# Two-layer transformer kernel: front of the second attention two sequences ahead, scores of two heads in row halves

## The chip, the cores and the metric

One core of one Trainium2 chip. The metric is the device time of the whole program in microseconds. A core has TensorE (PE; its weight loads stand apart as PEld), VectorE (DVE), ScalarE (ACT), GpSimd (POOL) and SyncE (SP), each with its own queue of instructions, and 16 DMA engines. Matmuls write to PSUM, eight banks of 512 f32 columns on 128 partitions.

## What is computed

16 sequences of 512 tokens and 128 channels, everything in f32, go through two layers. Each layer adds an attention and a feed-forward to its input:

```python
xn = layernorm(x)
x  = x + attn_A(xn) + block_B(xn)      # layer 0
xn = layernorm(x)
x  = x + flash_attn(xn) + fp4_ffn(xn)  # layer 1

# attn_A: 16 heads of 64; the mask keeps key position <= row position
k = einsum('ahe,bce->bach', W_K, x); q = einsum('ahe,bce->bach', W_Q, x); v = ...
scores = einsum('bach,baCh->bacC', k, q)            # rows are keys' tokens here
attn = softmax(masked(tril(scores)) / sqrt(64))
z = einsum('bach,bacC->baCh', v, attn); out = W_O z

# block_B: x + attn (layernorm, causal convolution of 3 taps, 16 heads of 8, rotary), then
#          x + mixture of 4 experts, each token uses the expert of its largest logit
# flash_attn: 16 heads of 8, blocks of 64 with a running maximum
# fp4_ffn: inputs and weights rounded to 4-bit values in groups of 16, gate/up/down 352 wide
```

## The kernel before

**Three parts of three sequences at a time.** The work on a sequence is cut into three parts, and `pipeline` runs them side by side for neighbours: in one call of `run(i, nxt, prv)` the sequence `i` is in its *dense* part (attn_A and the experts), `nxt` is in its *ahead* part (block_B's layernorms, convolution, second attention, router) and `prv` in its *behind* part (layer 1). The calls are one with `nxt` alone, one for sequence 0, a hardware loop (`Fori(1, B - 1)`, 14 passes), one for sequence 15 and one with `prv` alone. A period is one such call.

**Order by hand.** Every engine walks the same list in `walk`. The dense part has 129 places (0 to 63: 16 heads times four query tiles; 64 to 127: 16 chunks of the experts in four steps each); `PLACES` hangs the steps of the other two parts at places. Semaphores say what must be done; within an engine the order is the list's.

**First attention (dense, places 0 to 63).** For each head h, `key_side` projects `mg[h]` (W_Q and W_K multiplied in the preparation) with `xnTd` to a 128 x 512 tile in bank 3 (L1282); ACT copies it to `gs` (L661). Then four tiles t follow, with widths 128, 256, 384 and 512: a matmul of all 128 rows (L1325) into bank `pos % 3` and a bf16 mask matmul on its last 128 columns (L1327); DVE takes the row maxima (L976), ACT the exponentials and their sums (L681). The bank is free for the tile three places on when ACT is through. Every other head `value_side` projects v for a pair (L1273, bank 3, evacuated at L655); DVE inverts the sums (L937), POOL scales v (L550), and `values` multiplies (L1293, bank 4): the two heads of a pair write to partitions 0 to 63 and 64 to 127 of the bank, 64 columns of the array each. L1354 is the output projection `ao`.

**Experts (dense, places 64 to 127).** Per chunk a gate matmul (L1339), tanh on ACT (L694), two DVE operations (L947, L952) around a value matmul (L1346); the sums of each expert at L1305 and L963.

**Front of the second attention (ahead).** `load_x` (a DMA on ACT's queue into `xin`), `ln0_*`, `transpose0` (`xn` into `xnT`, later copied to `xnTd` at L645), `ln1_apply`, `transpose1`, `conv`, `project_q`/`project_k` with the rotation (two matmuls into banks 5 and 6), `split_q`/`split_k` (each value as a sum of three bf16 parts in `part`), and then 18 DMAs of 128 KB on POOL's queue (`send_stack`, L572), behind a tiny POOL operation each (L568), into `qst` and `kst`. These steps hang at places 1 to 12. `row_max` (44 units, L1399, L1401, L1041, banks 5 and 6) needs all 18 transfers and hangs at places 28 to 68; `shift_rows`, `exps` (44 units, L1418, L1420, L727) and `attend` (L1433, four heads in column quarters) lie in the expert places; then `divide`, `join`, `project_y`, `ln3_*`, `transpose3` (L1262), `route` (L1463).

**Behind.** `take_over` (L1096), `ln2_*`, `transpose2`, `keys1`, `queries1`, `values1`, `scores1`, `block_max1`, `shift1` (L1120), `sum1` (L1128), POOL's `totals1`, `blend1`, `weigh1`, then `probs_T1`, `mix1` (L1519), the 4-bit rounding (`round_x`, `round_h`) and `gate1`, `up1`, `transpose_hq`, `down1`. The result is stored by a DMA on ACT's queue (L790), and DVE waits for its landing at the end of the call.

## Time and profile before

| | before |
|---|---|
| median of 3 runs | 3992.66 us (3991.66 to 3997.45) |
| the profiled execution | 3994.44 us |
| its span, first to last instruction | 3992.6 us |
| PE busy | 3586.5 us (90%), 20335 matmul records |
| DVE busy | 2576.8 us (65%) |
| ACT busy | 1802.0 us (45%) |
| POOL busy | 608.3 us (15%) |
| mean granted clock of PE | 0.936 |

Times are in us unless marked ns; "L1325" is a line of the kernel. An f32 matmul stands as two records. The end of a matmul is modelled and lies behind its last column, so neighbouring records overlap: what a matmul costs is read from its start to the start of the next. The granted clock is 1 at 2.4 GHz and 0.5 at 1.2 GHz. "issue" as a releaser is idle time in which the engine waited for nothing that the profile shows.

### The profile page before, as it was taken

Reading aid. Unit: us, or ns where it says so; the run is one execution under the profiler, and the core shown is the slowest. Engines: PE = TensorE matmul, PEld = TensorE weight load, DVE = VectorE, ACT = ScalarE, POOL = GpSimd, SP = SyncE. Lnnn points to the kernel's source line nnn. Section 1 sums busy time; section 2 is a strip of 40 time slices with the busy share of each in tenths; the row PEclk is TensorE's granted clock in tenths of the full one; section 3 lists DMA queues with packets and bytes.
Section 4 is the critical chain, followed back from the end, with each engine's and each line's share of the span. In section 5 each row is a group of like instructions: output and inputs, shape, how many; then the busy total and the mean of one; then the engine's idle time right before and its main releaser. Section 6 shows DMA issues by size and latency. Waiting matters only on the chain.

```text
span 3992.6 us, 66986 instructions
## 1 busy us (share of the span) xinstructions
PE 3586.5 (90%) x20335; PEld 2096.9 (53%) x20335; DVE 2576.8 (65%) x6166; ACT 1802.0 (45%) x4300; POOL 608.3 (15%) x1188
## 2 busy tenths in 40 slices
PE   3799998999999899999989999998999999899974
PEld 2355554555555455555555555555555555555542
...
GB/s 98 4 25 4 25 2 31 2 13 19 6 27 2 31 2 7 25 5 27 2 31 2 7 25 5 27 2 31 2 12 20 5 28 2 31 2 4 1 3 3
DMA packets 51980, 59.15 MB, mean 15 GB/s; under 512 B 19634, under 2 KB 41076, under 8 KB 51572
## 3 DMA queue, kind: packets, MB, share of 16 engines
...
## 4 chain that ended last, share of the span: by engine, by line
PE 79%; DVE 9%; issue 6%; ACT 3%; POOL 2%; DMA 1%; SPq 1%; ACTq 0%; DVEq 0%; POOLq 0%
PE ps L1325 13%; PE ps L1282 6%; PE ps L1339 6%; PE ps L1293 6%; PE ps L1346 5%; PE ps L1305 5%; PE ps L1433 4%; PE ps L1418 4%; PE ps L1399 4%; PE ps L1273 3%; PE ps L1519 3%; PE ps L1497 3%; PE ps L1354 3%; PE ps L1513 1%; PE ps L1420 1%
## 5 line engine op out<-in xcount | busy, mean ns | idle before, releaser
L681 ACT ACTIVATE share_a<-ps,nma 128x128 f32<-128x128 f32 (+3 forms) x1024 | 539.1, 528 | 547.2 <-DVE nma L976 536.3
L1325 PE MATMUL ps<-share_g,xnTd 128*128 128x128 f32 (+3 forms) x2048 | 757.7, 467 | 30.6 <-ACT share_a L681 16.7
L976 DVE TENSOR_REDUCE nma<-ps 128x1 f32<-128x128 f32 (+3 forms) x1024 | 490.7, 488 | 397.9 <-PE ps L1327 382.5
L727 ACT ACTIVATE share_z<-ps 128x512 f32<-128x512 f32 (+1 forms) x704 | 369.3, 558 | 497.4 <-PE ps L1420 494.2
L1041 DVE TENSOR_REDUCE nmx<-ps 128x1 f32<-128x384 f32 (+3 forms) x704 | 427.0, 635 | 122.7 <-PE ps L1401 117.9
L1325 PEld LDWEIGHTS ps<-share_g,xnTd 128*128 128x128 f32 x2048 | 343.0, 198 | 267.7 <-issue 138.7
L947 DVE SCALAR_TENSOR_TENSOR share_g<-share_g,ps 128x512 f32<-128x512 f32 x256 | 175.3, 685 | 405.3 <-ACT share_g L694 403.4
L550 POOL TENSOR_TENSOR vn<-va,rla 128x256 f32<-128x256 f32 x256 | 160.3, 627 | 1277.7 <-DVE rla L937 1277.5
L1282 PE MATMUL ps<-xnTd,mg 128*128 128x512 f32 x512 | 307.4, 685 | 23.1 <-ACT va L655 23.1
L1293 PE MATMUL ps<-share_a,vn 128*64 128x512 f32 (+3 forms) x2048 | 309.8, 445 | 18.3 <-POOL vn L550 18.3
L577 POOL TENSOR_TENSOR share_s<-q1T,tab 128x1024 f32<-128x1024 f32 x16 | 30.4, 1899 | 1768.7 <-ACT q1T L755 1768.7
L1399 PE MATMUL ps<-kst,qst 96*128 96x128 bf16 (+3 forms) x1024 | 263.8, 311 | 29.1 <-DMA kst<-share_r 25.1
L1339 PE MATMUL ps<-h2Td,wgv 128*128 128x512 f32 x512 | 272.2, 613 | 19.0 <-ACT share_a L681 19.0
L1346 PE MATMUL ps<-h2Td,wgv 128*128 128x512 f32 x512 | 266.6, 602 | 0.0
L1418 PE MATMUL ps<-qst,kst 99*128 99x512 bf16 (+3 forms) x1024 | 255.1, 303 | 8.3 <-DMA qst<-share_h 4.2
L1293 PEld LDWEIGHTS ps<-share_a,vn 128*64 128x64 f32 x2048 | 138.0, 138 | 225.0 <-issue 192.1
L1305 PE MATMUL ps<-wdn,share_a 128*128 128x128 f32 x2048 | 251.9, 278 | 1.3 <-DVE share_a L952 1.3
L1305 PEld LDWEIGHTS ps<-wdn,share_a 128*128 128x128 f32 x2048 | 237.4, 192 | 13.4 <-issue 7.4
L1327 PE MATMUL ps<-up_b,ident_b 128*128 128x128 bf16 x1024 | 228.8, 223 | 0.0
L694 ACT ACTIVATE share_g<-ps 128x512 f32<-128x512 f32 x256 | 153.4, 599 | 124.8 <-PE ps L1339 123.8
L1401 PE MATMUL ps<-up_b,ident_b 128*128 128x128 bf16 x1024 | 202.8, 225 | 0.0
L655 ACT COPY va<-ps 128x512 f32<-128x512 f32 x128 | 74.7, 583 | 280.1 <-PE ps L1273 280.1
...
## 6 DMA issues: line engine op xcount, KB each, us to landing
qst<-share_r POOLq DMA_DIRECT2D x144, 128.0 KB, 7.3
kst<-share_r POOLq DMA_DIRECT2D x144, 128.0 KB, 12.7
xin<-in_L_attn_x ACTq DMA_DIRECT2D x16, 256.0 KB, 2.7
out<-xn ACTq DMA_DIRECT2D x16, 256.0 KB, 2.3
...
```

What stands on the lines that cost most here:

```text
L681: activation(pa[:, h % 4, OFF[t]:OFF[t] + P * (t + 1)], ps[:, pos % 3, 0:P * (t + 1)], ACT.Exp, bias=nma[:, h, t:t + 1], accum_out=la[:, h ...
L727: activation(pt[:, n % 2, h % 4:h % 4 + k, 0:wd], src, ACT.Exp, scale=SCALE_B)\
L976: v.tensor_reduce(nma[:, h, t:t + 1], ps[:, pos % 3, 0:P * (t + 1)], AX.X, ALU.max, negate=True).then_inc(amax, 1)
L1041: v.tensor_reduce(nmx[:, h:h + k, t], src, AX.X, ALU.max, negate=True).then_inc(bmax_ready, 1)
L1282: mm(ps[:, 3, :], mg[:, h, :], xnTd[:, :], start=True, stop=True).then_inc(g_psum, 1)
L1293: ins = mm(ps[DA * k:DA * k + DA, 4, 0:P * (t + 1)], vn[:, h % 4, t, :], pa[:, h % 4, OFF[t]:OFF[t] + P * (t + 1)], start=(t == NT - 1), s ...
L1305: ins = mm(ps[:, 3, tile(t)], ym[:, e % 2, c, tile(t)], wdn[:, e, c, :], start=(c == 0), stop=(c == CHUNKS - 1))
L1325: mm(ps[:, b, 0:P * (t + 1)], xnTd[:, tile(t)], gs[:, h % 2, 0:P * (t + 1)], start=True, stop=False)
L1339: mm(ps[:, (2 * n) % 3, :], wgv[:, e, c * P:(c + 1) * P], h2Td[:, :], start=True, stop=True).then_inc(gate_psum, 1)
L1346: mm(ps[:, (2 * n + 1) % 3, :], wgv[:, e, DFF + c * P:DFF + (c + 1) * P], h2Td[:, :], start=True, stop=True).then_inc(value_psum, 1)
L1399: mm(ps[:, b, o:o + wd], qst[0:SHIFT_ROW, h, tile(t)], kst[0:SHIFT_ROW, h, 0:wd], start=True, stop=False)
L1418: mm(ps[:, b, o:o + wd], kst[0:SHIFT_ROW + PARTS, h, tile(j)], qst[0:SHIFT_ROW + PARTS, h, j * P:T], start=True, stop=False)
```

## The change

**Pipeline.** A fourth part, *early*, is cut off the front of *ahead*: `load_x`, `ln0_*`, `ln1_apply`, `transpose1`, `conv`, `project`, `split` and the 18 stack transfers are done for the sequence two ahead (`nn`). `run(i, nxt, nn, prv)` is called once with `nn` alone, once with `nxt` and `nn`, for sequences 0 and 1, in the loop `Fori(2, B - 2)` (12 passes), for 14 and 15, and with `prv` alone.

**Order.** `PLACES` and the 129 places are gone; one list `ORDER` holds the steps of all four parts, the dense ones too. The early steps now stand among the expert steps; `row_max` 0 to 43 among the scores of pairs 1 to 7.

**First attention per pair.** The preparation keeps W_K and W_Q transposed (`wkqT`) and no product. Keys and queries of a pair of heads are projected in two matmuls (128 x 512 each) into two banks and copied together by one ACT operation 1024 wide. A unit of scores is a tile t of both heads: head 0 multiplies rows 0 to 63, head 1 rows 64 to 127 of the pair's `kq`, each into its own bank, then two mask matmuls. One DVE reduction takes both heads' maxima, two ACT operations the exponentials. The four banks 0 to 3 are a ring of two slots of two banks, through which projections and scores go in turn. `v` goes through bank 4, which it shares with `values`; one reciprocal and one POOL operation per pair take the place of two.

**Buffers and queues.** `xnT` and its copy go: `xn` is kept by a DMA in `xk`, transposed late in the period (`turn_x`) and written straight to `xnTd`. `hc`, `part`, `xres` and `kq_odd` have memory of their own (`kq_odd` doubles as `rope`). The loads of x (one into `xin`, one into `xres`), the 18 stack transfers, the copy to `xk` and the store of the result are on SP's queue; POOL and ACT issue no DMA. The wait for the store's landing moves from the end of DVE's call to the next `ln2_apply`.

```diff
-            run(None, (0, 0), None)
-            run((0, 0), (0, 1), None)
-            with eng.Fori(1, B - 1) as i:
-                run((i, 0), (i, 1), (i, -1))
-            run((0, B - 1), None, (0, B - 2))
-            run(None, None, (0, B - 1))
+            run(None, None, (0, 0), None)
+            run(None, (0, 0), (0, 1), None)
+            run((0, 0), (0, 1), (0, 2), None)
+            run((0, 1), (0, 2), (0, 3), (0, 0))
+            with eng.Fori(2, B - 2) as i:
+                run((i, 0), (i, 1), (i, 2), (i, -1))
+            run((0, B - 2), (0, B - 1), None, (0, B - 3))
+            run((0, B - 1), None, None, (0, B - 2))
+            run(None, None, None, (0, B - 1))
...
+RING = [("kq", 0), ("kq", 1)]
+for _p in range(PAIRS):
+    RING += [("scores", _p, _t) for _t in range(NT)] + ([("kq", _p + 2)] if _p + 2 < PAIRS else [])
+RING_AT = {unit: n for n, unit in enumerate(RING)}
...
+ORDER = [
+    ("take_over",), ("begin",), ("kq", 0), ("v", 0), ("kq", 1), ("ln2_stats",), ("scores", 0, 0), ("v", 1),
+    ("scores", 0, 1), ("ln2_root",), ("project_v",), ("scores", 0, 2), ("scores", 0, 3), ("ln2_apply",),
+    ("kq", 2), ("scores", 1, 0), ("transpose2",), ("scores", 1, 1), ("norm", 0), ("scores", 1, 2), ("keys1",),
+    ("z", 0), ("queries1",), ("row_max", 0), ("row_max", 1), ("values1",), ("v", 2), ("row_max", 2),
...
+    ("kq", 4), ("running_max1",), ("shift1", 0), ("scores", 3, 0), ("shift1", 1), ("shift1", 2), ("scores", 3,
+    1), ("norm", 2), ("row_max", 15), ("scores", 3, 2), ("z", 2), ("v", 4), ("shift1", 3), ("sum1", 0),
+    ("sum1", 1), ("sum1", 2), ("scores", 3, 3), ("sum1", 3), ("totals1", 1, 4), ("totals1", 4, 8), ("kq", 5),
+    ("row_max", 16), ("row_max", 17), ("row_max", 18), ("scores", 4, 0), ("row_max", 19), ("scores", 4, 1),
+    ("norm", 3), ("ratios1",), ("blend1", 7, 4), ("scores", 4, 2), ("blend1", 3, 0), ("row_max", 20),
+    ("row_max", 21), ("weigh1", 0), ("weigh1", 1), ("z", 3), ("row_max", 22), ("row_max", 23), ("v", 5),
+    ("scores", 4, 3), ("row_max", 24), ("row_max", 25), ("kq", 6), ("row_max", 26), ("row_max", 27),
+    ("probs_T1", 0, 0), ("weigh1", 2), ("scores", 5, 0), ("row_max", 28), ("scores", 5, 1), ("norm", 4),
...
+    ("round_h", 3, 3), ("round_h", 3, 4), ("ln3_root",), ("ln3_apply",), ("down", 3), ("acc", 3),
+    ("transpose_hq", 3), ("down1",), ("transpose3",), ("route",),
+]
...
# SP
+                def split(z):
+                    if z == 0 and nxt is not None:
+                        sp.wait_ge(bst_psum, count(nxt, AHEAD["bst_psum"], UNITS))
+                    stack = (qst, kst)[z]
+                    for a in range(PARTS):
+                        sp.wait_ge(split_ready, count(nn, EARLY["split_ready"], 3 * z + a + 1))
+                        for b in range(PARTS):
+                            r = DB * (PARTS * a + b) if z == 0 else DB * (PARTS * b + a)
+                            sp.dma_start(stack[r:r + DB, :, :], part[:, z, a, :]).then_inc(stack_loaded, 16)
...
# TensorE
+                def ring_turn(*unit):
+                    n = RING_AT[unit]
+                    if n >= 2:
+                        kind, p, *t = RING[n - 2]
+                        if kind == "kq":
+                            pe.wait_ge(kq_ready, count(i, DENSE["kq_ready"], p + 1))
+                        else:
+                            pe.wait_ge(aexp_done, count(i, DENSE["aexp_done"], 8 * p + 2 * t[0] + 2))
...
+                    return 2 * (n % 2)
+                def project_kq(p):
+                    if p == 0:
+                        pe.wait_ge(xnTd_ready, count(i, DENSE["xnTd_ready"], 1))
+                    b = ring_turn("kq", p)
+                    for z in range(2):
+                        ins = mm(ps[:, b + z, :], wkqT[:, z, 2 * DA * p:2 * DA * (p + 1)], xnTd[:, :],
+                                 start=True, stop=True)
+                    ins.then_inc(kq_psum, 1)
...
+                def scores(p, t):
+                    if t == 0:
+                        pe.wait_ge(kq_ready, count(i, DENSE["kq_ready"], p + 1))
+                    b = ring_turn("scores", p, t)
+                    for k in range(2):
+                        rows = slice(DA * k, DA * k + DA)
+                        mm(ps[:, b + k, 0:P * (t + 1)], kq[p % 2][rows, 0, tile(t)], kq[p % 2][rows, 1, 0:P * (t + 1)],
+                           start=True, stop=False)
+                    for k in range(2):
+                        ins = mm(ps[:, b + k, tile(t)], ident_b[:, :], up_b[:, :], start=False, stop=True)
+                    ins.then_inc(as_psum, 1)
...
-                        mm(ps[:, b, 0:P * (t + 1)], xnTd[:, tile(t)], gs[:, h % 2, 0:P * (t + 1)],
-                           start=True, stop=False)
-                        mm(ps[:, b, tile(t)], ident_b[:, :], up_b[:, :], start=False, stop=True).then_inc(as_psum, 1)
...
# VectorE
+                def scores(p, t):
+                    dve.wait_ge(as_psum, count(i, DENSE["as_psum"], 4 * p + t + 1))
+                    b = 2 * (RING_AT["scores", p, t] % 2)
+                    v.tensor_reduce(nma[:, 2 * p:2 * p + 2, t], ps[:, b:b + 2, 0:P * (t + 1)],
+                                    AX.X, ALU.max, negate=True).then_inc(amax, 1)
...
# ScalarE
+                    for k in range(2):
+                        h = 2 * p + k
+                        activation(pa[:, h % 4, OFF[t]:OFF[t] + P * (t + 1)], ps[:, b + k, 0:P * (t + 1)], ACT.Exp,
+                                   bias=nma[:, h, t:t + 1], accum_out=la[:, h, t:t + 1]).then_inc(aexp_done, 1)
```

## Rows read from the trace of the kernel before

**Rows 1.** The page, section 1: busy us, share of the span, instructions.
```profile
PE 3586.5 (90%) x20335; PEld 2096.9 (53%) x20335; DVE 2576.8 (65%) x6166; ACT 1802.0 (45%) x4300; POOL 608.3 (15%) x1188
```
**Rows 2.** The page, section 4: shares of the chain that ended last.
```profile
PE 79%; DVE 9%; issue 6%; ACT 3%; POOL 2%; DMA 1%; SPq 1%; ACTq 0%; DVEq 0%; POOLq 0%
```
**Rows 3.** The chain in order of time: start us, us, what; L1354.
```profile
1706.59 7.15 PE ps L1354 x64
1939.50 7.15 PE ps L1354 x64
```
**Rows 4.** Busy time by stretch: attention, experts, seam, prologue.
```profile
core 0: us, PE busy (x) PEld busy (x) DVE busy (x) ACT busy (x) POOL busy (x), PEclk, DMA share, GB/s
2028.00:2160.00 132.00, 123.10 (x632) 70.04 (x632) 97.41 (x227) 68.92 (x184) 37.21 (x73) 0.97 0.20 21
2160.00:2258.00 98.00, 93.48 (x635) 58.04 (x635) 62.76 (x157) 42.84 (x85) 0.70 (x1) 0.99 0.02 5
2021.00:2040.00 19.00, 11.26 (x43) 7.00 (x43) 11.65 (x55) 5.25 (x12) 0.00 (x0) 0.73 0.08 23
51.00:181.00 130.00, 76.55 (x448) 31.27 (x449) 48.17 (x107) 29.24 (x55) 12.56 (x24) 0.67 0.20 19
```
**Rows 5.** Timeline of PE, scores of one head: start us, us, what.
```profile
2085.91 1.08 PE L1325 MATMUL ps<-share_g,xnTd 128*128 128x512 f32 x2
2086.82 0.22 PE L1327 MATMUL ps<-up_b,ident_b 128*128 128x128 bf16 x1
2086.93 0.48 PE L1325 MATMUL ps<-share_g,xnTd 128*128 128x128 f32 x2
2087.25 0.22 PE L1327 MATMUL ps<-up_b,ident_b 128*128 128x128 bf16 x1
```
**Rows 6.** Timeline of PE, the values of one pair.
```profile
2102.78 0.22 PE L1327 MATMUL ps<-up_b,ident_b 128*128 128x128 bf16 x1
2102.93 2.38 PE L1293 MATMUL ps<-share_a,vn 128*64 128x512 f32 x16
2105.23 0.34 PE L1399 MATMUL ps<-kst,qst 96*128 96x384 bf16 x1
```
**Rows 7.** Groups by line and shape: busy us, mean ns, idle before, releaser.
```profile
L976 DVE TENSOR_REDUCE nma<-ps 128x1 f32<-128x512 f32 x256 | 176.6, 690 | 100.9 <-PE ps L1327 95.0
L976 DVE TENSOR_REDUCE nma<-ps 128x1 f32<-128x128 f32 x256 | 73.5, 287 | 120.5 <-PE ps L1327 115.9
L681 ACT ACTIVATE share_a<-ps,nma 128x512 f32<-128x512 f32 x256 | 175.7, 686 | 263.4 <-DVE nma L976 263.4
L681 ACT ACTIVATE share_a<-ps,nma 128x128 f32<-128x128 f32 x256 | 95.1, 371 | 56.5 <-DVE nma L976 53.3
L681 ACT ACTIVATION_READ_ACCUMULATOR share_a<-ps,nma 128x1 f32 x1024 | 201.0, 196 | 0.0
```
**Rows 8.** Timeline of PE at a seam in the loop; last line: the first seam.
```profile
2024.12 1.05 PE L1463 MATMUL ps<-wrt,share_h 128*128 128x4 f32 x8 [0.87 <-ACT share_h L741]
2028.29 2.07 PE L1273 MATMUL ps<-wvT,xnTd 128*128 128x128 f32 x8 [3.12 <-issue]
2031.04 2.07 PE L1282 MATMUL ps<-xnTd,mg 128*128 128x512 f32 x2 [0.68 <-ACT va L655]
...
2039.76 0.65 PE L1262 MATMUL ps<-ident,xn 128*128 128x128 f32 x4 [1.68 <-DVE xn L844]
...
383.82 1.14 PE L1273 MATMUL ps<-wvT,xnTd 128*128 128x128 f32 x8
```
**Rows 9.** Waits: engine, line, waited for, us in total, times, longest.
```profile
PE ps L1399 <- DMA kst<-share_r: 25.1, 2, 23.8
PE ps L1293 <- POOL vn L550: 18.3, 5, 7.5
...
POOL qst L572 <- issue: 17.0, 3, 7.8
```
**Rows 10.** The page, section 6: DMA issues, KB each, us to landing.
```profile
qst<-share_r POOLq DMA_DIRECT2D x144, 128.0 KB, 7.3
xin<-in_L_attn_x ACTq DMA_DIRECT2D x16, 256.0 KB, 2.7
```

659 lines of the change are left out of this document (327 added, 332 removed), and 10 rows, old and new, of tables (ORDER, PLACES).

## Prediction

> **What bounds the kernel now.** I read the page's busy shares first: TensorE (PE) is busy 90% of the span, VectorE (DVE) 65%, ScalarE (ACT) 45% [rows 1]. A busy PE need not be the bound, so next the chain of work that ended last: 79% of it is PE, 9% DVE [rows 2]. So I sum PE time. The steady state repeats: the output projection of the first attention (64 records, L1354) starts every 233 us [rows 3]; sixteen of these are 93% of the time. Three stretches of one period come next [rows 4]: the attention stretch (132 us: PE 123, DVE 97), the expert stretch (98 us: PE 93, DVE 63), and the seam between two sequences (19 us: PE only 11.3, granted clock 0.73). At two levels, 2.4 and 1.2 GHz, a mean of 0.73 means that a good half of those 19 us ran at the lower one. So there are two things to win: PE work inside the period, and the seam.
>
> **Scores in row halves.** An f32 matmul stands as two records. 64 records of 128 columns take 7.15 us [rows 3], so 0.223 us for 128 columns and 2.23 us for the 1280 columns of one head's four tiles (128+256+384+512). Measured by starts, a head takes 0.91 us for its 512-column tile and 0.32 us for its 128-column tile [rows 5], which lies nearer to 2.4 for the head. Two heads, one after the other, are then 4.46 to 4.80 us; the masks (0.06 us each, same number) stay. The nearest row for two half-array matmuls side by side is the product with the values (L1293), which lies in column halves: eight f32 matmuls, 2560 columns, the same number as two heads of scores. They start 0.15 us after a mask where 0.06 is usual, and the next instruction starts 2.30 us later [rows 6]: 2.39 us, not 4.46. So halves do run side by side, and a visit to the split array costs about 2.39 - 2.23 = 0.16 us (up to 0.26 if I take a faster column rate). After the change the rows are halved and not the columns, an operation that the trace does not show. There are four visits per pair and not one, because the full-array masks stand behind each tile. A pair costs 2.23 + 4 x 0.16 = 2.87 us at best, 2.13 + 4 x 0.26 = 3.2 us at worst. Saved: between 1.3 and 1.9 us per pair; I take 1.45, since a short visit can hide less of its weight load. 16 sequences of 8 pairs: 186 us (range 165 to 245). The new projections `project_kq` have 2 x 512 columns per pair, as had the two `key_side`: nothing.
>
> The Trainium skill ("TensorEngine Tiling (Array Packing)", Tiling Modes, Key Properties) says that changing the tiling mode drains the TensorE, which speaks against four visits per pair; the 0.09 us of late start in rows 6 agrees with a drain of that size. The same page allows row halves to run independently if they write different PSUM banks (Gotcha 1), as here; no row shows that yet.
>
> **The ring of score banks.** Before: three banks, one head each. After: two slots of two banks, and the projections take slots too. A slot is free when both heads' exponentials are through. Price of a slot's return: a reduce of both heads (128 columns 0.29, 512 columns 0.69 us, so 0.42 to 1.23 us for double width by that slope), then two exponentials with their accumulator reads (0.46 to 0.78 us each by start) [rows 7], plus some 0.35 us of PE drain (a 0.06 us mask stands as 0.22, rows 5) and hops: 1.7 us for tile 0, 3.2 us for tile 3. Beside it PE has one other unit (0.6 to 1.2 us) and what the order puts between. I walked pair 4 and 5 of the new order: between tile 0 and tile 2 of pair 4 there are only one `row_max` (0.28) and tile 1 (0.8), against 1.7 plus a DVE queue: 0.7 us of idle. Pair 3 has `shift1` and `sum1` on DVE (eight operations 1024 wide, about 1.2 us each by the same slope) and 13.7 us of DVE against 10.6 of PE: some 3 us. Pair 5 comes through without a wait. DVE in the attention stretch after the change: 97 (rows 4) + 2 (the last `row_max`) - 5 (eight pairs of 3.3 for 3.9 us) - 16 (`ln0`, convolution, rotation and splits leave, some 24 operations of 0.4 to 0.7 us and 30 small ones beside) = about 78 us of about 115, so DVE binds only where its work is bunched. I price the ring at +4 us per sequence against 1 to 2 now; ends: 1 (the walk counts waits that other work fills) and 10 (each pair waits 1.2 us).
>
> **The seam.** Now [rows 8]: 0.87 us for the activation in front of the router, then 3.12 us with nothing to wait for, then 0.68 us for the evacuation of v (a like one of g follows) and 1.68 us for `ln2_apply`. The 3.12 us are there only in the loop: at the first, unrolled seam the same L1273 follows with no idle [rows 8]. It is the jump back, and the change keeps a loop (12 passes, not 14), so 3.1 us stay. `xnTd` no longer comes through two copies behind the route; `kq` 0, `v` 0 and `kq` 1 stand in a row (4.4 us), so the waits for v and g go. But tile 2 of pair 0 and `kq` 2 wait for DVE, which has `route`, `take_over`, `begin`, `ln2_stats` and `ln2_root` (about 8 us of small operations) in front of the reductions: I count 2 to 4 us. The idle stays near 8 us; denser work behind it should bring the clock back some 3 us of work earlier. The output store and the waits behind it leave ACT and the end of DVE's run, which gives little: the DVE idle there is the jump. I take 4 us per seam won, less the 2.5 us of the ring: net 2.5 us with the rest of the period's small waits, 16 times: 40 us.
>
> **The front two sequences ahead.** `ln0`, convolution, rotation, splits and 18 stack transfers per sequence move from the attention stretch into the expert stretch, where DVE has room (63 of 98 us) [rows 4]. PE does the same matmuls. The stack goes from POOL's queue to SP's. SP waits there for the last `exps`; behind it in its queue stand the copy `xk` and the output store, neither needed before the next `turn_x` and `ln2_apply`. The transfers (128 KB, 7.3 us each for the queries, overlapping) [rows 10] made PE wait 23.8 us in the prologue [rows 9]; from the last `exps` to the next `row_max` 0 I count about 50 us of PE work. Hidden; without that cover up to 24 us a sequence. POOL also loses its long idle pieces at the transfers, with no releaser shown (17.0 us in three at the query stack alone); behind them PE waited for POOL's `vn` for 18.3 us in sum [rows 9]: I take 15 us.
> The prologue grows: sequence 0's front runs alone as now, but sequence 1's front is now in the stage behind it. There the PE clock is 0.67 and DVE is busy 48 of 130 us [rows 4], so most of some 20 us of DVE work hides: +12 us (0 to 20), of which the end gives back nothing, since the last period is set by other work. The tail, the second block of the last sequence alone, has no part in the change.
>
> **Sum.** The profiled execution has a span of 3992.6 us and 3994.4 us in all, 1.8 around it; the median shown is 3992.7. 3994 - 186 - 40 - 15 + 12 = 3765 us.
>
> **Rivals.**
> A. The halves don't overlap, or the mode change eats the gain (slower). Row halves are not column halves: if both heads' partial sums go down the same columns one after the other, a pair costs 4.46 + 4 x 0.16 = 5.1 us, 2.1 more than the forecast pair of 3.0 to 3.1, 128 times: 270 us, so 4035. The same side is reached from 0.56 us per visit (2.23 / 4). Against it: rows 6. Its neighbour: the stack transfers on one queue one after the other (18 x 7.3 = 131 us against 50 of cover), which would cost over 50 us a sequence; against it, a 256 KB load on ACT's queue lands in 2.7 us [rows 10]. 11% together.
> B. The ring binds: each pair waits 1.2 us more, and DVE with its bunches keeps PE from running ahead: +6 us per sequence, 3860. For it: two slots, and `row_max` in front of reductions. 18%.
> C. Better: visits at 0.16, serial heads at 2.4, the walk's waits filled, clock at the seam up. 40 us more from the scores, 4 us a period: 3665. 14%.
> D. The change of place matters nothing and the scores give half, since a short tile's weight loads show: 3870 to 3950, close to B. 4%, with 2% of no change at all.
> The forecast's own case: 51%, 3700 to 3820.
>
> **How the numbers follow.** 3765 is the likeliest. The range reaches over B and most of C and leaves A out: 3660 to 3925. One measurement of this kernel can tell about 0.2% from no change. Faster by more: the forecast, B, C and D, 0.87; within: 0.02; slower: 0.11.
>
> **What would show it.** Scores: the two heads' records start within some ns of each other, and a pair of tiles of 128 to 512 columns with its masks takes 3.3 to 3.7 us. If the second head starts only when the first is through, A. Ring: PE's waits for the exponentials and evacuations of the first attention come to 40 to 100 us in sum; over 150 is B. Seam: about 8 us idle in 19, the 3.1 us still there in the loop. Period: 219 us, not 233. Stack: no PE wait for `kst` beyond the prologue's. DVE near 155 us of 219. The prediction is wrong in kind if a period stays above 230 us.

## The result, and the profile after

The changed kernel takes 3896.1 us (median; 3885.1 to 3904.0) beside 3992.2 us of the kernel before: a ratio of 0.9756, 95% interval 0.9743 to 0.9768. That is 96 us less. The forecast was 3765 us, 227 us less: the sign and the range held, the size did not. The profiled execution of after took 3885.1 us (span 3883.0). It is the fastest of its four, 11 us under the median, at a mean granted clock of 0.941 where the other three have 0.937; the one of before took 3994.4 us.

The busy shares of the page, which answer to [rows 1]:

```profile
PE 3406.5 (88%) x20319; PEld 1876.6 (48%) x20319; DVE 2506.9 (65%) x5526; ACT 1754.1 (45%) x4156; POOL 381.3 (10%) x676
```

PE lost 180 us of busy time, the span only 110: PE was busy for 90% of the span and now for 88%. POOL lost 227 us, DVE 70.

Next one period in one window. Columns as in [rows 4]; idle is the width less PE's busy time. First before, from one value projection (L1273) to the next:

```profile
core 0: us, PE busy (x) PEld busy (x) DVE busy (x) ACT busy (x) POOL busy (x), PEclk, DMA share, GB/s
2491.90:2724.50 232.60, 219.32 (x1268) 129.54 (x1268) 158.55 (x383) 111.98 (x268) 37.92 (x74) 0.96 0.12 14
```

232.6 us, of which PE idles 13.3. Three periods of after, from one output projection (L1403) to the next:

```profile
1647.20:1871.90 224.70, 208.12 (x1268) 115.58 (x1267) 154.46 (x343) 108.89 (x259) 23.82 (x42) 0.97 0.11 17
1871.90:2100.90 229.00, 211.38 (x1269) 116.60 (x1268) 154.67 (x344) 108.90 (x259) 23.83 (x42) 0.96 0.12 16
2100.90:2323.70 222.80, 205.57 (x1269) 114.91 (x1268) 154.42 (x344) 108.85 (x259) 23.83 (x42) 0.98 0.12 17
```

They are 224.7, 229.0 and 222.8 us wide, with 16.6, 17.6 and 17.2 us idle. Counted from one sequence's first value projection (L1349) to the next one's, the ten periods behind the loop's first pass have a mean of 225.8 us; the forecast was 219. In the three windows PE is busy for 8 to 14 us less in a period, at a granted clock of 0.96 to 0.98 (0.96 before), and idles 3 to 4 us more, where the forecast had it idle less. In 15 periods 136 us are won. The first value projection starts at 201.2 us instead of 181.2, so the prologue gives back 20 us (12 forecast), and the end 6.

The scores, PE's timeline, one tile of 512 columns and one of 128, each for both heads of a pair (as [rows 5], where each was one head):

```profile
2486.95 1.13 PE L1359 MATMUL ps<-kq_odd 64*128 64x512 f32 x4
2488.01 0.29 PE L1362 MATMUL ps<-up_b,ident_b 128*128 128x128 bf16 x2
2488.14 1.94 PE L1337 MATMUL ps<-xnTd,wkqT 128*128 128x512 f32 x4
...
2491.44 0.22 PE L1462 MATMUL ps<-up_b,ident_b 128*128 128x128 bf16 x1
2491.59 0.49 PE L1359 MATMUL ps<-share_g 64*128 64x128 f32 x4
2492.01 0.29 PE L1362 MATMUL ps<-up_b,ident_b 128*128 128x128 bf16 x2
2492.14 0.38 PE L1460 MATMUL ps<-kst,qst 96*128 96x512 bf16 x1
```

From start to start a wide tile of both heads with its two masks is 1.19 us and a narrow one 0.55 (two heads, one after the other, by [rows 5]: 2 x 1.02 and some 2 x 0.43). The halves overlap. Behind another mask a tile starts 0.15 us after it where 0.06 is usual, as in [rows 6]. With the two tiles between (0.76 and 0.97) and four late starts of 0.09 a pair takes 3.82 us; the prediction looked for 3.3 to 3.7.

The seam in the loop, PE, ACT and DVE (answers to [rows 8]; the last bracket is the idle time in front and what ended it):

```profile
2418.39 1.06 PE L1524 MATMUL ps<-wrt,share_h 128*128 128x4 f32 x8 [0.87 <-ACT share_h L777]
...
2422.65 3.53 PE L1337 MATMUL ps<-xnTd,wkqT 128*128 128x512 f32 x4 [3.21 <-issue]
...
2429.33 0.62 ACT L692 COPY h2Td<-share_h 128x512 f32<-128x512 f32 x1 [10.99 <-issue]
...
2430.99 0.49 PE L1359 MATMUL ps<-share_g 64*128 64x128 f32 x4 [2.19 <-ACT share_g L703]
...
2431.62 0.43 DVE L1147 COPY xp<-xacc 128x512 f32<-128x512 f32 x1 [10.19 <-issue]
```

PE waits behind the jump as before (3.21 us, 3.12 then). New is that ACT's and DVE's first instructions behind it come 10.99 and 10.19 us late, also without a releaser. The evacuation of `kq` 0 stands behind ACT's, so `scores` 0,0 (L1359) waits 2.19 us. The 19 us around this jump, and the same 19 us of the kernel below that sends the transfers from POOL, to be set beside the third row of [rows 4]:

```profile
2415.30:2434.30 19.00, 12.73 (x66) 8.35 (x66) 7.08 (x33) 3.71 (x5) 0.00 (x0) 0.87 0.53 79
1490.60:1509.60 19.00, 14.64 (x80) 9.23 (x78) 9.84 (x46) 6.79 (x15) 0.00 (x0) 0.82 0.22 50
```

PE idles 6.3 us in the one and 4.4 in the other, against 7.7 before, at a clock of 0.87 and 0.82 against 0.73. In the mean of ten seams it is 7.3 us before, 6.0 after and 4.2 with POOL's transfers. So the seam itself did get better; the jump's late engines took back some 2 us of it.

Waits (engine, what, for whom: us in sum, times, longest), which answer to [rows 9]:

```profile
PE ps L1359 <- ACT share_a L718: 56.8, 70, 1.9
PE ps L1337 <- issue: 47.3, 11, 11.8
PE ps L1460 <- DMA kst<-part: 36.4, 1, 36.4
PE ps L1376 <- POOL vn L614: 35.0, 48, 1.8
...
PE ps L1337 <- ACT share_a L718: 22.8, 16, 1.9
...
ACT h2Td L692 <- issue: 111.0, 11, 11.0
...
DVE xp L1147 <- issue: 100.7, 11, 10.3
```

The copies behind the jump waited 10.1 and 9.2 us in the mean, in each of 11 passes; before it was 38.4 us in 13 for DVE. PE's longest wait at the jump, 11.8 us, stands in the loop's first pass, which is 232.2 us long. The prologue waits 36.4 us for the stack (23.8 before), and POOL's `vn` holds PE up 48 times for 35.0 us (18.3 in 5 before).

### The profile page after: what moved, and what is told of

The parts are those of the page before. It is cut to its first block, busy times and chain, and to the rows that moved or that the text cites. A ratio compares the mean times of both kernels' runs of the same rounds, so it can differ in the third digit from the quotient of the medians.

```text
span 3883.0 us, 62655 instructions
## 1 busy us (share of the span) xinstructions
PE 3406.5 (88%) x20319; PEld 1876.6 (48%) x20319; DVE 2506.9 (65%) x5526; ACT 1754.1 (45%) x4156; POOL 381.3 (10%) x676
## 4 chain that ended last, share of the span: by engine, by line
PE 68%; DVE 12%; issue 8%; POOL 6%; ACT 5%; SPq 1%; DMA 1%; POOLq 0%; DVEq 0%; ACTq 0%
PE ps L1376 7%; PE ps L1394 5%; PE ps L1359 5%; PE ps L1387 5%; PE ps L1415 5%; PE ps L1494 4%; PE ps L1479 4%; PE ps L1558 3%; PE ps L1337 3%; PE ps L1580 3%; PE ps L1403 3%; DVE nma L1020 2%; PE ps L1460 2%; PE ps L1349 2%; POOL vn L614 2%
## 5 line engine op out<-in xcount | busy, mean ns | idle before, releaser
L1020 DVE TENSOR_REDUCE nma<-ps 128x2 f32<-128x256 f32 (+3 forms) x512 | 420.8, 825 | 416.0 <-PE ps L1362 408.2
L614 POOL TENSOR_TENSOR vn<-va,rla 128x512 f32<-128x512 f32 x128 | 133.7, 1044 | 3060.7 <-DVE rla L976 3060.7
L1376 PE MATMUL ps<-share_a,vn 128*64 128x512 f32 (+3 forms) x2048 | 324.1, 461 | 37.1 <-POOL vn L614 35.0
L1337 PE MATMUL ps<-xnTd,wkqT 128*128 128x512 f32 x512 | 279.2, 672 | 70.1 <-issue 47.3
L1460 PE MATMUL ps<-kst,qst 96*128 96x128 bf16 (+3 forms) x1024 | 264.5, 311 | 56.1 <-DMA kst<-part 36.4
L1359 PE MATMUL ps<-kq_odd 64*128 64x128 f32 (+3 forms) x1024 | 216.7, 501 | 41.6 <-ACT share_a L718 35.5
L993 DVE SCALAR_TENSOR_TENSOR share_a<-share_g,ps 128x512 f32<-128x512 f32 x256 | 175.7, 686 | 105.1 <-PE ps L1394 96.9
L1359 PE MATMUL ps<-share_g 64*128 64x128 f32 (+3 forms) x1024 | 209.7, 486 | 29.9 <-ACT share_a L718 21.3
L718 ACT ACTIVATION_READ_ACCUMULATOR share_a<-ps,nma 128x1 f32 x1024 | 202.5, 198 | 0.0
L1462 PE MATMUL ps<-up_b,ident_b 128*128 128x128 bf16 x1024 | 201.5, 225 | 0.0
L1479 PEld LDWEIGHTS ps<-qst,kst 99*128 99x128 bf16 x1024 | 99.3, 98 | 205.2 <-ACT share_z L760 98.6
```

Of the source, the lines that this page charges most:

```text
L718: activation(pa[:, h % 4, OFF[t]:OFF[t] + P * (t + 1)], ps[:, b + k, 0:P * (t + 1)], ACT.Exp, bias=nma[:, h, t:t + 1], accum_out=la[:, h, ...
L1020: v.tensor_reduce(nma[:, 2 * p:2 * p + 2, t], ps[:, b:b + 2, 0:P * (t + 1)], AX.X, ALU.max, negate=True).then_inc(amax, 1)
L1337: ins = mm(ps[:, b + z, :], wkqT[:, z, 2 * DA * p:2 * DA * (p + 1)], xnTd[:, :], start=True, stop=True)
L1359: mm(ps[:, b + k, 0:P * (t + 1)], kq[p % 2][rows, 0, tile(t)], kq[p % 2][rows, 1, 0:P * (t + 1)], start=True, stop=False)
L1376: ins = mm(ps[DA * k:DA * k + DA, 4, 0:P * (t + 1)], vn[:, h % 4, t, :], pa[:, h % 4, OFF[t]:OFF[t] + P * (t + 1)], start=(t == NT - 1), s ...
L1460: mm(ps[:, b, o:o + wd], qst[0:SHIFT_ROW, h, tile(t)], kst[0:SHIFT_ROW, h, 0:wd], start=True, stop=False)
```

## The experiments

Three questions: what do the stack's transfers cost, what does DVE's bunch in the attention stretch cost, and what are the row halves worth? The kernel times below are medians of four runs; the ratios are to the kernel before, 3993 to 3995 us in the same sessions, with intervals of 0.0016 to 0.0023 (6 to 9 us) to each side.

Means of the ten periods behind the loop's first pass (for the kernel before, its 4th to 13th period), worked out over the traces; each is of one execution:

| kernel | period, us | PE idle, us | granted clock |
|---|---|---|---|
| before | 233.8 | 14.6 | 0.962 |
| after | 225.8 | 17.8 | 0.973 |
| small transfers | 225.2 | 15.5 | 0.963 |
| transfers from POOL | 224.9 | 15.8 | 0.966 |
| transfers of 16 rows from SP | 225.4 | 15.5 | 0.962 |
| from POOL, new order | 225.3 | 14.9 | 0.956 |
| from POOL, full rows | 228.8 | 13.6 | 0.985 |
| from POOL, light block steps | 220.9 | 13.8 | 0.979 |
| the same with full rows | 226.7 | 11.7 | 0.986 |

### The stack transfers

**Smaller.** Each transfer carries an eighth of its bytes:

```diff
-    sp.dma_start(stack[r:r + DB, :, :], part[:, z, a, :]).then_inc(stack_loaded, 16)
+    sp.dma_start(stack[r:r + 1, :, :], part[0:HEADS, z, a, :]).then_inc(stack_loaded, 16)
```

> Each of the 18 stack transfers carries an eighth of its bytes (one row of eight; the first sequence's stay whole, so the output is wrong after it), with every semaphore and wait in place. Theory J (the transfers, which run across the loop's jump, slow the start of each engine behind it): the first copies behind the jump wait 10.1 us (ACT, 111.0 in 11) and 9.2 us (DVE, 100.7 in 11) now; they fall to the 2 to 3 us of the kernel before, TensorE's own wait there falls from 4.3 us to 3.1, and a period falls by 3 to 4 us from 225.4: 15 of them give 45 to 60 us, 3836 to 3850 us. Rival S (the seam costs what TensorE's own jump and clock cost; the late copies are hidden): under 10 us, 3885 to 3900.

Measured: 0.9679 (3865 us), 31 us faster than the changed kernel, between the two theories.

```profile
DVE xp L1150 <- issue: 32.9, 11, 3.2
...
PE ps L1340 <- issue: 34.4, 11, 3.5
```

DVE's wait falls to 3.0 us a pass and PE's longest to 3.5. So the late start of the engines behind the jump does come from transfers under way. In the traces, which are 21 us apart, half of the gain lies in one place, the loop's first pass (232.2 to 221.2 us); the ten periods behind it go from 225.8 to 225.2 only. One of them:

```profile
1509.30:1735.10 225.80, 209.94 (x1268) 116.41 (x1267) 154.78 (x347) 109.08 (x259) 23.77 (x42) 0.96 0.03 8
```

By the table PE idles 2.3 us less in such a period, and the lower clock (0.963 against 0.973) took most of that back. But this is the fastest execution of after. Its other three have the same mean clock over the whole run as the four with small transfers (0.937 against 0.936 to 0.939) and are 28 us or more slower than these. So the mechanism was right, and its price was set too high: 3 to 4 us a period by the theory, 0.6 us in the traces, and some 2 us of idle time where the clocks are alike. Why the clock of the one execution was higher, no run shows.

**Behind the jump.** All 18 are issued by SP at the start of the next pass, ahead of its other transfers:

```diff
-    if z == 0 and nxt is not None:
-        sp.wait_ge(bst_psum, count(nxt, AHEAD["bst_psum"], UNITS))
+    if z == 0 and i is not None:
+        sp.wait_ge(carried, count(i, DENSE["carried"], 1))
+        sp.wait_ge(bst_psum, count(i, AHEAD["bst_psum"], UNITS))
...
```

> The same 18 transfers, whole, but issued by SP behind the jump (when the dense copy of x is made), not ahead of it. Theory J: the waits behind the jump fall as with small transfers, and the transfers (some 24 us) land 27 to 32 us behind the seam, where the first row maximum is due at 26.4 us: 3 us a sequence gained at the jump, 0 to 4 lost at the first row maximum, 3840 to 3910 us, with a row for row_max waiting for kst or qst. Rival S: nothing gained at the jump, the wait for the stack alone: 3900 to 3960.

Measured: 1.0505 (4193 us), far outside of both. SP's issues, and the first row maximum of the same period:

```profile
2635.93 6.20 SPq L567 DMA_DIRECT2D qst<-part  x9
2642.24 16.87 SPq L567 DMA_DIRECT2D kst<-part  x9
```
```profile
2677.87 0.29 PE L1462 MATMUL ps<-kst,qst 96*128 96x128 bf16 x1 [20.04 <-DMA kst<-part]
```

From the first issue at 2635.9 to the end of PE's wait at 2677.9 are 42 us. SP's row of 6.2 + 16.9 us is the time of issue, not of landing. The ten periods behind the loop's first pass have a mean of 246.0 us, 20 more than after. I had taken the prologue's wait of 23.8 us for the length of the transfers, twice.

The 9 of the keys alone behind the jump, those of the queries where they were:

```diff
     if z == 0 and nxt is not None:
         sp.wait_ge(bst_psum, count(nxt, AHEAD["bst_psum"], UNITS))
+    if z == 1 and i is not None:
+        sp.wait_ge(carried, count(i, DENSE["carried"], 1))
...
```

> The changed kernel with the 9 transfers of the key stack issued by SP behind the jump, those of the query stack ahead of it as before. 18 took 43 us to land, so 9 should take about 21: the first half is over ahead of the jump, the second lands 4 + 21 = 25 us behind the seam, where the first row maximum is due at 26.4. Theory J: the copies behind the jump wait 2 to 3 us instead of 9 to 11, as with small transfers, the loop's first pass loses its 11.8 us wait, and the time comes out like that kernel's, 3855 to 3880 us, with at most 1 us a period for row_max. If it comes out at 3900 or above, transfers that run behind the jump cost in another way, or take longer than half.

Measured: 0.9759 (3896 us), no gain, outside of the expected 3855 to 3880. Behind the jump ACT waits 1.9 us and DVE 3.0, as expected, and the ten periods behind the loop's first pass are 225.2 us. But at the first two seams, which are unrolled, the first row maximum comes before the keys and waits 3.2 and 4.6 us; the second of them stands in the loop's first pass, which stays at 231.5 us. The three unrolled periods are 4, 6 and 8 us longer, and the second pass of the loop still waits 1.3 us. That eats the gain.

**From POOL's queue**, as in the kernel before. With each group stands the small `turn` operation of the kernel before:

```diff
-    sp.dma_start(stack[r:r + DB, :, :], part[:, z, a, :]).then_inc(stack_loaded, 16)
+    nc.gpsimd.dma_start(stack[r:r + DB, :, :], part[:, z, a, :]).then_inc(stack_loaded, 16)
```

> The changed kernel with all 18 stack transfers issued by POOL, as the kernel before does, instead of SP. In the first sequence they landed 28 us behind their first issue from POOL and 43 us from SP. Theory J with this rate: the wait for the stack in the prologue falls from 36.4 to about 22 us (14 us), and in the loop the transfers are over 28 us behind 2387.5, ahead of the jump at 2419, so the late copies behind the jump go as with small transfers (31 us there): 3845 to 3865 us. Rival: POOL's ring of descriptors (a quarter of the size in the kernel before) throttles the issues, and they land no sooner than SP's: 3880 to 3910.

Measured: 0.9634 (3849 us), 47 us faster than the changed kernel, at the expected place. It does the full work and is the fastest such kernel of this study.

```profile
PE ps L1475 <- DMA kst<-part: 26.0, 1, 26.0
...
DVE xp L1162 <- issue: 33.3, 11, 3.2
...
1500.40:1725.70 225.30, 209.96 (x1269) 116.15 (x1268) 154.50 (x344) 109.18 (x259) 35.44 (x66) 0.96 0.13 17
```

The prologue's wait falls by 10 us, the late copies behind the jump are gone. The period shown is 225.3 us at a clock of 0.96, like the one with small transfers. The traces are 35 us apart: 10 us ahead of the first value projection, 9 in the loop's first pass, 9 in the ten periods behind it. One thing still differs from the kernel before: the changed kernel sets `dynamic_dma_scratch_size=4096`, which that one leaves alone. POOL stands 10.0 us with no releaser in front of its tenth transfer; whether the setting does that, no run shows.

**SP's queue, another shape.** The same bytes in the same pieces, but 16 of the 18 transfers write 16 rows of 8 heads instead of 8 rows of 16:

```diff
-    sp.dma_start(stack[r:r + DB, :, :], part[:, z, a, :])
+    n = PARTS * a + b      # n < 8; the ninth keeps its 8 rows
+    dst = stack[16 * (n // 2):16 * (n // 2) + 16, 8 * (n % 2):8 * (n % 2) + 8, :]
+    sp.dma_start(dst, part[:, z, a, :])
```

> The changed kernel, all stack transfers from SP, of the same bytes and the same 1 KB pieces, but 16 of the 18 write 16 rows of 8 heads where they wrote 8 rows of 16 heads (the stacks' layout is wrong, and with it the output). The windows show SP's transfers at a DMA share of 0.49 to 0.57 and 57 to 60 GB/s, POOL's at up to 0.98 and 104 GB/s. Theory E (SP's transfer with 8 outer rows runs on half of the DMA engines): share near 1 and over 90 GB/s, 18 transfers land in some 25 us instead of 43, the prologue's wait for the stack falls from 36.4 to about 20 us and the copies behind the jump wait 2 to 3 us: 3845 to 3865 us. Rival (SP's queue itself is slow, whatever the shape): 3885 to 3905 us. The Trainium skill (DMA: Bandwidth & Descriptors, Why a DMA increments its semaphore by 16 and not by 1) says that a transfer is spread over the largest number of engines up to 16 that divides the slowest dimension of both sides, which here would be 8 and 16; what follows from it is theory E.

Measured: 0.963 (3847 us), as fast as from POOL's queue and in the range of theory E. DMA share and GB/s are the last two columns; after first, behind its first issue:

```profile
2388.00:2400.00 12.00, 11.48 (x78) 7.85 (x78) 8.54 (x22) 4.05 (x9) 0.00 (x0) 1.00 0.53 61
2400.00:2411.00 11.00, 9.56 (x52) 6.19 (x51) 10.02 (x31) 2.38 (x5) 0.00 (x0) 1.00 0.57 58
```

and with 16 rows:

```profile
1458.00:1470.00 12.00, 11.48 (x77) 7.72 (x77) 8.41 (x22) 4.18 (x9) 0.00 (x0) 1.00 1.04 111
1470.00:1482.00 12.00, 10.56 (x61) 7.19 (x60) 10.95 (x33) 2.38 (x5) 0.00 (x0) 1.00 1.00 101
```
```profile
PE ps L1464 <- DMA kst<-part: 20.3, 1, 20.3
...
ACT h2Td L696 <- issue: 21.4, 11, 2.2
...
DVE xp L1151 <- issue: 32.8, 11, 3.2
```

Half of the engines' time and 58 to 61 GB/s in the one, all of it and 101 to 111 GB/s in the other. So SP's queue is not slow by itself; a transfer with 8 outer rows ran at half rate. This is what the Trainium skill gives ("DMA: Bandwidth & Descriptors", Why a DMA increments its semaphore by 16 and not by 1): a transfer is spread over the largest number of engines, at most 16, that divides the slowest dimension of both sides. The trace agrees with it for 8 and for 16. The same passage says that such a transfer takes the lowest-numbered engines from SP and a moving set from POOL; that would explain why POOL's 8-row transfers landed sooner, and no run here shows the single engines.

### DVE's bunch in the attention stretch

In the period of the kernel with POOL's transfers, the 30 us with the second layer's block maxima, shifts and sums, and the 30 behind them:

```profile
1542.00:1572.00 30.00, 24.53 (x127) 11.07 (x125) 25.17 (x39) 17.39 (x43) 5.41 (x18) 0.89 0.01 1
1572.00:1602.00 30.00, 29.71 (x194) 16.21 (x190) 17.08 (x28) 17.12 (x47) 12.28 (x19) 1.00 0.00 1
```

DVE is busy 25.2 of 30 us and PE idles 5.5; behind it, 17.1 and 0.3. How that comes about, timeline:

```profile
1545.70 2.28 DVE L1174 TENSOR_REDUCE bm<-share_s 128x32 f32<-128x2048 f32 x1
...
1548.10 1.23 DVE L1035 TENSOR_REDUCE nma<-ps 128x2 f32<-128x1024 f32 x1
...
1549.36 0.69 ACT L733 ACTIVATE share_a<-ps,nma 128x512 f32<-128x512 f32 x1 [2.53 <-DVE nma L1035]
...
1550.86 0.30 PEld L1374 LDWEIGHTS ps<-kq_odd 64*128 64x128 f32 x4 [2.50 <-ACT share_a L733]
```

A block maximum of 2.28 us, then the reduction of scores 2,3, then its exponentials, and `scores` 3,0 waits 1.68 us for them: a ring of two slots.

**Short readers.** In the loop the maximum and the exponentials of the scores read 128 columns only:

```diff
-    ps[:, b:b + 2, 0:P * (t + 1)]
+    ps[:, b:b + 2, 0:P]
```

> In the 12 passes of the loop the maximum of the dense scores and their exponentials read the first 128 columns only (wrong output), so the release of a ring bank comes 0.3 to 1.4 us sooner for the wider tiles, while TensorE's work is unchanged. Theory R (the ring of two pairs of banks is late because its readers are long): stalls over 0.35 us in the attention stretch, 8.6 us a period now, fall to about 3: 5 to 6 us in 12 periods, 3825 to 3840. Rival O (they come from the places of single steps: a block maximum of 2.3 us ahead of a reduction, values waiting for vn, values waiting for the evacuation of z): 1 to 3 us a period, 3860 to 3885.

Measured: 0.9574 (3825 us), 71 us faster, at the edge of theory R. It doesn't tell a slow ring from a crowded DVE, since it lightens both.

**Light block steps**, the ring left as it is:

```diff
-    v.tensor_reduce(ll[:, 2 * k:2 * k + 2, :], ss[:, 2 * k:2 * k + 2, :, :], AX.X, ALU.add)
+    v.tensor_reduce(ll[:, 2 * k:2 * k + 2, :], ss[:, 2 * k:2 * k + 2, :, 0:16], AX.X, ALU.add)
```

and so for the block maxima and the shifts; ACT's exponentials of the same tiles keep their width and take a scale divided by 64.

> On the kernel with the transfers from POOL: block maxima, shifts and sums of the second layer read and write a quarter of their columns (wrong output), in their places: DVE's burst loses 9.9 us of its 13.3 (2 times 2.28, 4 times 1.22, 4 times 1.21, but for a fixed part), TensorE's and ACT's work is the same. Theory D: the stalls at 49 to 70 us behind the seam (5.2 us) fall to 1 or 2 us and the clock's fall of 6.8 us there goes: 5 to 7 us a period, 3745 to 3775 us. Rival R (the ring is late with or without the burst): under 2 us a period, 3820 to 3849.

Measured: 0.9440 (3772 us), 77 us faster than its base. The same 30 us:

```profile
1520.40:1550.40 30.00, 26.35 (x162) 12.96 (x162) 19.73 (x43) 20.36 (x54) 8.38 (x29) 1.00 0.00 1
```

DVE 19.7, idle 3.7, and the clock 1.00 instead of 0.89: theory D's range. In the traces, 74 us apart, 58 us lie in the 15 periods (3.9 each), 7 in the last sequence's scores and experts, and 9 behind them, in the last call, where no scores run. So beside the scores the bunch costs some 4 us a sequence, in idle time and in clock. The kernel before has the same block steps, and no run lightens them there: how much of these 4 us the change brought isn't shown.

**Spreading it at full work.** The lines of these five diffs are the ones that the reading rests on; each list moves more steps than are shown (12, 50, 23, 20 and 8, against the list that it starts from). The first, on the changed kernel:

```diff
-    ("block_max1", 1), ("v", 3), ("scores", 2, 3)
+    ("v", 3), ("scores", 2, 3), ("block_max1", 1)
-    ("scores", p + 1, 1), ("norm", p)
+    ("scores", p + 1, 0), ("norm", p)
-    ("gate1", 3), ("gate", 15), ("up1", 3), ("value", 15)
+    ("gate", 15), ("gate1", 3), ("value", 15), ("up1", 3)
-    ("transpose_hq", 3), ("down1",), ("transpose3",)
+    ("transpose_hq", 3), ("transpose3",), ("down1",)
```

> The changed kernel with eleven steps placed anew, same work: the second block maximum behind the scores (2,3), so that the reduction of (2,3) doesn't stand behind its 2.3 us on DVE; each reciprocal (norm) ahead of the other DVE steps between two pairs; value projection 4 behind scores (3,3); gate 15 ahead of gate1 3 and up1 3 behind value 15; transpose3 ahead of down1. Theory O (the period's stalls above 0.3 us are set by single steps' places: 1.68, 1.37, 0.55, 0.68, 1.31 and 1.44 us of 17.5 idle): 5 to 6 us of idle gone in each of 15 periods, one fall of the clock in the attention stretch gone too, 3790 to 3825 us. Rival F (the same stalls come back a step later, since DVE and ACT are late as a whole, or the clock gives the gain back): under 2 us a period, 3865 to 3895.

Measured: 0.9799 (3913 us), 17 us slower, beyond even rival F's 3895. The waits of 1.37 and 1.31 us went, but one of 2.67 came before `scores` 3,2, and 1.34 and 2.74 at `transpose_hq` 3 and `transpose3`.

The same order with the transfers from POOL:

> Both: the transfers from POOL and the steps placed anew. If their causes are separate, the gains add: about 40 us of the one and 70 to 100 of the other, 3750 to 3790 us. If the clock or the late engines give one back, it stays near the better of the two.

Measured: 0.9652 (3855 us), 6 us above POOL's transfers alone, which is within the intervals: the order adds nothing there either. By the table PE idles 0.9 us less in a period, but at a clock of 0.956 instead of 0.966.

Next, on POOL's transfers, shifts and sums with a score tile between them, and row maxima at the seam:

```diff
-    ("ln2_apply",), ("kq", 2), ("scores", 1, 0)
+    ("ln2_apply",), ("row_max", 0), ("row_max", 1), ("kq", 2), ("row_max", 2), ("scores", 1, 0)
-    ("z", 2), ("v", 4), ("shift1", 3), ("sum1", 0), ("sum1", 1), ("sum1", 2), ("scores", 3, 3)
+    ("z", 2), ("shift1", 1), ("scores", 3, 3), ("v", 4), ("shift1", 2)
+    ("scores", 4, 0), ("sum1", 0), ("norm", 3), ("scores", 4, 1), ("sum1", 1), ("scores", 4, 2)
```

> On the kernel with the transfers from POOL (3849 us): the attention stretch's steps placed by DVE's load. In that kernel's trace DVE is busy 25.0 of the 30 us in which the block maxima, shifts and sums of the second layer stand (48 to 58% elsewhere in the stretch), and TensorE idles 4.9 of them at a granted clock of 0.89. Here shifts and sums are spread over two pairs of heads, each with one score tile between, and row maxima 0 to 3 go up to the seam, where TensorE waits 1.9 us and DVE is half idle. Theory D (the burst on DVE is what stalls TensorE): idle of that stretch and the 1.9 us fall from 7.1 us to 2 or 3, the falls of the clock behind them (10.2 us in a period) go in part: 5 to 8 us a period, 3730 to 3775 us. Rival F (stalls move and the clock takes back what is gained, as with the first reordering): 3835 to 3865.

Measured: 0.9921 (3963 us), far above both theories. The longest of its new waits, 8.0 us in every period of the loop:

```profile
PE ps L1391 <- POOL vn L614: 146.4, 31, 8.1
```

`norm` 4 stood behind other work in POOL's queue, which I had not walked.

Then with that place mended, and others moved with it:

```diff
-    ("weigh1", 0), ("weigh1", 1), ("norm", 4)
+    ("norm", 4), ("weigh1", 0), ("weigh1", 1)
-    ("block_max1", 1), ("norm", 2)
+    ("norm", 2), ("block_max1", 1)
```

> As the spread placement before it, with its one bad place mended: there the vector of pair 4 (norm 4) stood on POOL behind the ratios, the blend and two weighings, and the values of pair 4 waited 8.0 us for it in every period; here norm 4 stands ahead of the weighings and norm 2 ahead of the block maximum. That kernel without its 8.0 us and 1.8 us would be 222.5 us a period, against 225.1 of the kernel with the transfers from POOL (3849 us). Theory D (the burst on DVE): 2.5 to 6 us a period under 3849, 3760 to 3815 us. Rival F (what goes in one place comes back in another): 3840 to 3870.

Measured: 0.9811 (3919 us), again above both: `v` 4 waits 2.6 us, `z` 4 2.8, the transposed probabilities 1.8.

A smaller spread:

```diff
-    ("sum1", 0), ("sum1", 1), ("sum1", 2), ("scores", 3, 3), ("sum1", 3), ("kq", 5)
+    ("sum1", 0), ("scores", 3, 3), ("v", 4), ("sum1", 1), ("kq", 5), ("sum1", 2)
+    ("scores", 4, 0), ("norm", 3), ("sum1", 3)
```

> On the kernel with the transfers from POOL: only the shifts and sums spread (sums 1 to 3 behind scores (3,3), kq 5 and scores (4,0)), norm 2 and 3 ahead, row maxima 0 and 1 at the seam and row maximum 14 between kq 4 and scores (3,0), where TensorE waits 1.68 us. Theory D: the stalls at 49 to 60 us behind the seam (4.0 us) fall to 1.5, the one of 1.89 to 1: 3 to 5 us a period with the clock, 3775 to 3805 us. Rival F: 3840 to 3870.

Measured: 0.9798 (3912 us), above both once more, and again one queue in POOL. The wait is 6.0 us in a period; the 26.7 us are of the last call:

```profile
PE ps L1589 <- POOL share_s L653: 117.1, 16, 26.7
```

And with the two first weighings ahead of `norm` 4:

```diff
-    ("weigh1", 0), ("scores", 5, 0), ("norm", 4), ("weigh1", 1), ("weigh1", 2)
+    ("weigh1", 0), ("weigh1", 1), ("scores", 5, 0), ("norm", 4), ("weigh1", 2), ("weigh1", 3)
```

> The small spread (3912 us) with its one bad place mended: there the first transposes of the probabilities waited 6.0 us in each period for the second weighing on POOL, which stood behind norm 4, and POOL itself waited 5.2 us for the ratios. Here the ratios stand ahead of scores (4,3), both first weighings ahead of norm 4, and the four transposes one score tile later. Without the 6.0 us a period of that kernel (228.9) is 222.9, against 225.1 of the kernel with the transfers from POOL (3849 us). Theory D: 1 to 3 us a period under it, 3805 to 3835 us. Rival F (the chain from the block maxima to the probabilities has no slack, so whatever is spread ahead of it stalls TensorE behind it): 3845 to 3880.

Measured: 0.9654 (3856 us) with that place mended: rival F, and not faster than its base (3849). Waits of 1.7 and 1.1 us now stand where the probabilities are transposed and mixed. None of these orders was faster than the one that the change has, on the same queue. The work behind the bunch (sums on DVE, totals, ratios and weighings on POOL, transposes on PE) follows so closely that each delay ahead of it showed behind it. That no order is better isn't shown.

### What the row halves are worth

The same edit on three bases, the scores over all 128 rows, one head after the other:

```diff
-    rows = slice(DA * k, DA * k + DA)
+    rows = slice(0, 2 * DA)
```

> The scores' matmuls read all 128 rows for each head, so two heads no longer overlap in row halves and no change of mode is left (the scores of both heads of a pair come out as their sum); the rest of the changed kernel stands. Streams from the trace: a tile of both heads .427, .853, 1.28, 1.71 us against .424, .635, .848, 1.06, and about .09 us less at each entry: a pair 4.75 us against 3.81, 7.5 us a sequence. Theory P (TensorE is still what bounds the attention stretch, and the gain of the row halves was real): 6 to 8 us a sequence slower than the changed kernel, 3990 to 4025 us, which puts the rest of the change at about nothing. Theory R (the ring or the order binds and eats the gain): 0 to 3 us a sequence, 3890 to 3945.

Measured on the changed kernel: 0.9891 (3952 us), so the halves are worth 56 us. It lies between the theories; part of the difference is other:

```profile
PE ps L1337 <- issue: 75.8, 11, 11.9
```

against 47.3 us in the changed kernel. The trace of this one is of the slowest of its four runs (3968 us), the other of the fastest, so of the 28 us only a part belongs to the medians.

> On the kernel with the transfers from POOL: the scores' matmuls read all 128 rows, one head after the other (output is the sum of two heads). Without the long waits at the jump, which stood in 5 of 12 passes of the first such kernel. Streams cost 7.5 us a sequence more; its undisturbed passes were 230.9 us against 225. Theory P (the row halves are worth what is left of their stream after the stalls they bring): 5 to 6 us a sequence, 3930 to 3945 us. Rival: the full 7.5 us (3965 to 3975), if the stalls beside the scores have nothing to do with how fast they stream.

Measured on the kernel with POOL's transfers: 0.9776 (3905 us), 56 us above its base, 3.5 us a sequence, under both expectations. The same two tiles, and a period:

```profile
1597.06 1.88 PE L1374 MATMUL ps<-share_g 128*128 128x512 f32 x4
1598.78 0.28 PE L1377 MATMUL ps<-up_b,ident_b 128*128 128x128 bf16 x2
1598.89 0.27 PE L1475 MATMUL ps<-kst,qst 96*128 96x256 bf16 x1
...
1602.12 0.61 PE L1374 MATMUL ps<-kq_odd 128*128 128x128 f32 x4
1602.56 0.28 PE L1377 MATMUL ps<-up_b,ident_b 128*128 128x128 bf16 x2
1602.67 0.33 PE L1475 MATMUL ps<-kst,qst 96*128 96x384 bf16 x1
```
```profile
1500.00:1728.60 228.60, 215.49 (x1269) 127.44 (x1268) 154.92 (x346) 109.11 (x259) 37.03 (x69) 0.99 0.11 16
```

1.83 and 0.55 us against 1.28 and 0.64 (1.19 and 0.55, each with its late start): with 1.03 and 1.45 between, a pair of heads streams 4.86 us against 3.82, 8.3 us a sequence. But the full rows' period has only 13.1 us idle, and the clock is 0.99.

> The kernel with the light block steps (3772 us) with full rows in the scores: how much the row halves are worth when DVE's burst is gone. With the burst they were worth 56 us (3905 to 3849), 3.6 us a sequence, where their streams differ by 7.5. Theory D (the burst ate part of the difference): 5 to 7 us a sequence, 3855 to 3885 us. Theory C (the clock ate it: full rows are at the low clock for 6.8 us of a period, row halves for 17.1): again 50 to 60 us, 3820 to 3835.

Measured on the light block steps: 0.9702 (3875 us) against 3772: 103 us, 6.4 a sequence, theory D's range. With the bunch the halves give 56 us, without it 103, and by their streams 133. It would be wrong, though, to read this as idle time that the bunch adds: by the table the halves bring 2.2 us more idle a period with the bunch and 2.1 without it. What differs is the granted clock. It falls from 0.985 to 0.966 with the bunch, from 0.986 to 0.979 without it; at two levels that is 7 us of a period at the lower one growing to 15, against 6 growing to 9. So theories D and C exclude each other less than their ranges say: the total goes with D, and in the traces the bunch takes its part of the gain by way of the clock.

## Why the prediction was right and wrong

- **The direction, and rival A.** Right: the two heads overlap, so 4035 us was out. The Trainium skill ("TensorEngine Tiling (Array Packing)", Gotcha 1) has different row tiles write to different PSUM banks, since two can't access the same one at once. Here each head has its own bank, and the 1.19 us for a wide tile of both heads show that nothing else kept them apart.
- **The step that failed: the term of the scores (186 us).** It was counted as if all of the saved stream shortened the span. Undone by itself it is worth 56 us. A part of the miss is the stream: a pair is 3.82 us less 0.48 of masks less 2.23, so four visits cost 0.28 us each, where I priced 0.16 to 0.26, and against serial heads in the new order a pair saves 1.04 us and not 1.45 (133 us in all). The larger part is that only 56 of the 133 came through. By the table the halves bring 2.2 us more idle a period and a clock of 0.966 instead of 0.985. With DVE's bunch lightened 103 us come through.
- **The transfers, priced at nothing ("Hidden").** The second step that failed: they cost 47 us. I asked of the moved transfers only whether `row_max` would wait for them. It doesn't: some 42 us of landing, from 2387.5 us in the trace, lie ahead of the row maximum at 2449.1. They also lie across the jump, and there every engine starts late. "Up to 24 us" was one wait from POOL's queue, taken for the duration of 18 transfers from SP's.
- **The rest of the sum: right by luck.** With full rows the changed kernel takes 3952 us, so everything but the halves gave 41 us, and the other terms of the sum (40 + 15 - 12) come to 43. But with the transfers from POOL the same comparison gives 88 us (3905): the new pipeline and order won about twice what I had them win, and the transfers took half of it back. By the table that gain is clock more than idle time (0.985 against 0.962 before, 13.6 us idle against 14.6). The 2.5 us a sequence in the forecast hold 1 us "with the rest of the period's small waits", for which it shows no row.
- **The ring (+4 us a sequence, ends 1 and 10).** I walked pair 3 and saw its 13.7 us of DVE against 10.6 of PE and priced it at 3 us. The bunch costs some 4 us a sequence beside the scores; no run tells how much of that is new. The waits for exponentials and evacuations (56.8, 22.8 and others, 103 us) came out at the upper end of 40 to 100. `vn` was added to them (35.0 us, 18.3 before), where I had taken 15 us off.
- **The seam (-4 us).** The 3.1 us stayed as said, and the clock came up as said. The idle time in 19 us was to stay near 8 us; it is 6.0 in the mean of ten seams (7.3 before), and 4.2 where the transfers are over before the jump. What was missing is the late start of ACT and DVE.
- **The prologue (+12 us).** 20, of which the slower transfers are 10 to 15: the first value projection starts at 201.2 us, with the transfers from POOL at 190.7 and with 16 rows at 186.1, as the waiting falls from 36.4 us to 26.0 and 20.3.
- **Sum.** With the transfers from POOL and the bunch lightened the kernel is 221 us below before, near the 227 of the forecast. This is no proof of the sum: the lightened kernel does less work, and the kernel before has the bunch too.
- **Signs and rivals.** A pair 3.82 us (3.3 to 3.7 forecast); period 225.8 (219 forecast, 230 would have been wrong in kind); DVE 154.5 us of it (155 forecast); no PE wait for `kst` but the prologue's, as forecast. In time rival D (3870 to 3950, given 4%) came true, but not by its account: the change of place gave 41 us and not nothing, the scores 56 and not half of 186. Rival B, the ring at 3860, is 36 us off, and its sign, over 150 us of waits, was not met. No rival had the transfers delay the engines at the jump.
